# Two edits to one kernel: the last steps of the attention part written out by hand, and the Mish reciprocal computed by three squares and one cubic step in halves

## The chip, the cores and the metric

One core of a Trainium2 chip runs the whole kernel. The metric is the device time of one execution in microseconds (us), lower is better. The median of the kernel before is 1624.23 us over 3 runs, from 1624.13 to 1624.23.

## What is computed

The reference is a transformer-like block on 64 graphs of 128 nodes and 384 features, in float32. Cut to what matters:

```python
x = x + attention(layernorm(x), adj)        # 12 heads of 32, adj is added to the scores, softmax
x = x + moe(layernorm(x))                   # below, layernorm of its output with gain and offset

pooled = u.mean(axis=1)                     # one routing decision for each graph
logits = pooled @ router_w.T + router_b     # 4 experts, the best 2 are taken
h = act[e](u @ w1[e] + b1[e])               # 384 -> 768; act = gelu, silu, mish, gelu
out = h @ w2[e] + b2[e]                     # 768 -> 384
y = gate-weighted sum of the 2 + u
mish(v) = v * tanh(softplus(v))
```

## The kernel before

The kernel is written for each engine by hand, with semaphores between the engines. `act.wait_ge(s, n)` stops only that engine's own list until the semaphore `s` has reached `n`; what is behind it in the list waits too. Matrices are split in a high and a low part, and each product is three matmuls (`split_product`, L495).

**Attention part.** The loop `for h in STEPS` runs over the 64 graphs (B = 64, graphs 0 to 63) as a software pipeline: in step h an engine works on the scores of graph h, on the probabilities of graph h-1, on the output projection of graph h-2 and on the normalised tile `u` of graph h-3. The names are: `exps` (ScalarE, L776, 12 exponentials for a graph), `take_probs` (copy of the transposed probabilities, two of three tiles on ScalarE at L795, the third on VectorE at L1206), `take_inverse` (L806), `divide` (VectorE, L1225 to L1231), `project_o` (TensorE), `residual` (VectorE, L1196 to L1201), `root2` (GpSimd, L1073 to L1077), `normalise_x1` (ScalarE, L783, writes `u` into `xu`), `transpose_u` (TensorE, L601), `take_u` (ScalarE, L801), `sum_nodes` (VectorE, L1218). Each graph's `xu` (384 KB) is stored to DRAM from the SP queue (L425) and so is its transposed `u` (192 KB, L397).

**Weights under dead tiles.** The expert part's tiles lie over those of the attention part. As the last graphs leave tiles, ScalarE's DMA queue loads into them: four `w1_hi` parts of 1152 KB (L824), the bias `b1_wide` of 1536 KB (L844) and six pieces of `w2_both` (L829; 896, 1920, 2560, 1152, 768 and 1920 KB). The functions `load_under_...` hold the waits for that, and stand in ScalarE's list between its activations.

**Expert part.** There are 128 jobs, two for each graph: job (b, k). TensorE's list for a job is six transposes of an activated tile (`transpose_act`, L704), the 18 matmuls of `first_layer` of a later job, and the 18 of `second_layer` of this one. VectorE adds the bias (`take_hidden`, L1323), ScalarE and VectorE apply the activation, ScalarE and VectorE split the transposed tile in `at_hi` (L998) and `at_lo` (L1402). The expert of a job is read at run time, and `If` picks the activation. In this run 17 jobs are Mish jobs.

**The Mish job before.** ScalarE computes a tanh and a square that give the number whose reciprocal is wanted, and then a seed by two squares (L916, L1005). VectorE then does three operations on the whole 128x768 tile (L1430, L1433, L1437), with one square of ScalarE (L1007) beside the second, and at the end the product in two halves (L1441):

```python
nc.scalar.activation(inverse[:], inverse[:], ACT.Square, bias=seed_out[:]).then_inc(seed_done, 1)
act.wait_ge(miss_done, i + 1)
nc.scalar.activation(miss2[:], half_t[:], ACT.Square, scale=-1.0, bias=one_col[:]).then_inc(miss2_done, 1)
```

The first job, (0, 0), starts on ScalarE only when several things are there: the routing, the last output projection, and the stores of the `xu` tiles of graphs 60 and 61, over which its tiles lie (`xu_stored[0]`):

```python
act.wait_ge(routed, 1)
act.wait_ge(wo_mm, B)
for g in range(2):
    act.wait_ge(xu_stored[0][g], 16 * stored(0))
activate(0, 0, choice(0, 0))
```

## Time and profile before

| | |
|---|---|
| median of 3 runs | 1624.23 us |
| the profiled execution's own time | 1624.92 us |
| its span | 1623.0 us |
| granted TensorE clock, mean | 0.997 |
| busy: TensorE, VectorE, ScalarE, GpSimd | 1587.8, 1193.3, 971.5, 687.3 us |

The profiled execution is 0.69 us above the median, and 1.92 us of its time lie outside the span. Times in the views are microseconds from the span's start; durations in the grouped view are in nanoseconds. In a row of the timeline the bracket gives how long the engine sat idle before it and what released it. TensorE runs at 2.4 GHz where the granted clock reads 1.00, and at 1.2 GHz where it reads 0.50.

### The profile page before, as it was taken

Reading aid. Unit: us, or ns where it says so; the run is one execution under the profiler, and the core shown is the slowest. Engines: PE = TensorE matmul, PEld = TensorE weight load, DVE = VectorE, ACT = ScalarE, POOL = GpSimd, SP = SyncE. Lnnn points to the kernel's source line nnn. Section 1 sums busy time; section 2 is a strip of 40 time slices with the busy share of each in tenths; the row PEclk is TensorE's granted clock in tenths of the full one; section 3 lists DMA queues with packets and bytes.
Section 4 is the critical chain, followed back from the end, with each engine's and each line's share of the span. In section 5 each row is a group of like instructions: output and inputs, shape, how many; then the busy total and the mean of one; then the engine's idle time right before and its main releaser. Section 6 shows DMA issues by size and latency. Waiting matters only on the chain.

```text
span 1623.0 us, 44743 instructions
## 1 busy us (share of the span) xinstructions
PE 1587.8 (98%) x12720; PEld 1524.2 (94%) x12720; DVE 1193.3 (74%) x3752; ACT 971.5 (60%) x2882; POOL 687.3 (42%) x1105
## 2 busy tenths in 40 slices
PE   7999999999999999979999999999999999999998
PEld 7999999999999999879999999999999999999998
DVE  5788788878888788767766666776777767677776
ACT  6899999998999988853433333443444434343442
POOL 3777887778877887631111111111111111111112
PEclk9999999999999999999999999999999999999999
DMA  5433333344444433582111111122211111111211
GB/s 186 157 118 125 109 115 115 127 158 153 153 154 161 151 121 120 221 312 85 52 59 60 58 57 60 60 60 61 61 60 45 58 58 60 60 60 50 66 50 45
DMA packets 93511, 163.87 MB, mean 101 GB/s; under 512 B 10304, under 2 KB 73792, under 8 KB 92096
## 3 DMA queue, kind: packets, MB, share of 16 engines
q1 hardware_dynamic: 91664, 145.01, 27.3%
q10 hardware_dynamic: 1584, 15.73, 2.6%
q8 instruction: 119, 1.95, 0.5%
q14 instruction: 144, 1.18, 0.2%
HBM read 96.22 MB, written 64.49 MB: 99 GB/s over the span
## 4 chain that ended last, share of the span: by engine, by line
PE 88%; DVE 5%; ACT 2%; issue 2%; DMA 1%; POOL 1%; DVEq 1%; ACTq 0%; POOLq 0%; SPq 0%
PE bank L495 67%; PE bank L569 5%; PE bank L704 5%; PE bank L522 3%; PE bank L592 3%; PE bank L609 2%; PE bank L578 1%; PE bank L601 1%; DVE inverse L1437 1%; DVE half_t L1430 1%; DVE inverse L1433 1%; ACT inverse L1005 1%; ACT at_hi L998 1%; DMA xu_scratch<-xu 1%; ACT prob L776 1%
## 5 line engine op out<-in xcount | busy, mean ns | idle before, releaser
L495 PE MATMUL bank<-w_hi,ut_in 128*128 x1536 | 421.3, 341 | 0.1
L495 PE MATMUL bank<-w_both,at_hi 128*128 x1524 | 388.8, 335 | 8.0 <-DVE at_lo L1402 7.3
L776 ACT ACTIVATE prob<-att,heads 128x128 f32<-128x128 f32 x768 | 297.6, 394 | 15.0 <-DVE heads L1166 12.1
L495 PEld LDWEIGHTS bank<-w_both,at_hi 128*128 128x128 f32 x1524 | 274.3, 188 | 13.6 <-issue 13.6
L495 PEld LDWEIGHTS bank<-w_hi,ut_in 128*128 128x128 f32 x1536 | 279.5, 188 | 1.1 <-issue 1.1
L495 PE MATMUL bank<-w_lo,ut_in 128*128 x768 | 257.0, 335 | 0.0
L495 PE MATMUL bank<-w_both,at_lo 128*128 x762 | 255.1, 335 | 0.0
L920 ACT ACTIVATE hid<-hid 128x384 f32<-128x384 f32 x192 | 95.0, 526 | 257.1 <-DVE hid L1323 254.9
L998 ACT ACTIVATE at_hi<-bank,gate_col 128x384 fp32r<-128x384 f32 x254 | 133.4, 576 | 192.5 <-PE bank L704 190.5
L1142 POOL TENSOR_TENSOR xz<-xz,lnb_wide 128x384 f32<-128x384 f32 x64 | 67.9, 1062 | 403.7 <-DVE xz L1468 383.7
L1402 DVE SCALAR_TENSOR_TENSOR at_lo<-bank,gate_col,at_hi 128x384 fp32r<-128x384 f32 x254 | 144.7, 611 | 113.4 <-ACT at_hi L998 113.3
L1323 DVE TENSOR_TENSOR hid<-bank,b_wide 128x384 f32<-128x384 f32 x256 | 130.7, 552 | 118.1 <-PE bank L495 107.7
L1130 POOL TENSOR_SCALAR rs_z<-mv_z 128x1 f32<-128x1 f32 x64 | 40.8, 638 | 346.0 <-DVE mv_z L1456 346.0
L1166 DVE CUSTOM_DVE_ANT_0 att<-bank,adj_in 128x128 f32<-128x128 f32 x768 | 171.7, 286 | 12.5 <-PE bank L522 12.0
L495 PE MATMUL bank<-xt_hi,wt_hi 128*128 128x256 f32 x576 | 169.1, 294 | 0.1
L495 PE MATMUL bank<-xt_lo,wt_hi 128*128 128x256 f32 x576 | 162.6, 282 | 0.0
L495 PE MATMUL bank<-xt_hi,wt_lo 128*128 128x256 f32 x576 | 162.6, 282 | 0.0
L776 ACT ACTIVATION_READ_ACCUMULATOR prob<-att,heads 128x1 f32 x768 | 147.7, 192 | 0.0
L495 PEld LDWEIGHTS bank<-w_lo,ut_in 128*128 128x128 f32 x768 | 144.7, 188 | 0.0
L495 PEld LDWEIGHTS bank<-w_both,at_lo 128*128 128x128 f32 x762 | 143.0, 188 | 0.0
L1088 POOL TENSOR_TENSOR fold<-att 128x768 f32<-128x768 f32 x64 | 117.2, 1832 | 0.0
L495 PEld LDWEIGHTS bank<-xt_hi,wt_hi 128*128 128x128 f32 x576 | 109.6, 190 | 7.6 <-issue 0.4
(139 smaller groups left out, 3485.8 us busy)
## 6 DMA issues: line engine op xcount, KB each, us to landing
xu_scratch<-xu SPq DMA_DIRECT2D x64, 384.0 KB, 2.3
xz<-xu_scratch SPq DMA_DIRECT2D x64, 384.0 KB, 3.2
x_in<-in_x SPq DMA_DIRECT2D x32, 384.0 KB, 3.2
xu<-in_x SPq DMA_DIRECT2D x32, 384.0 KB, 4.2
ut_scratch<-ut_out SPq DMA_DIRECT2D x64, 192.0 KB, 1.9
ut_in<-ut_scratch SPq DMA_DIRECT2D x64, 192.0 KB, 2.4
out_dram<-xz SPq DMA_DIRECT2D x64, 192.0 KB, 1.9
w_lo<-in_L_ffn_w SPq DMA_DIRECT2D x4, 1152.0 KB, 6.3
```

What stands on the lines that cost most here:

```text
L495: last = nc.tensor.matmul(acc, lhs[c][a], rhs[c][b], start=start and n == 0, stop=stop and n == len(terms) - 1)
L522: last = nc.tensor.matmul(bank[r][:, c * N:(c + 1) * N], q_t[p][rows, c, cols], k_t[p][rows, c, cols], start=True, stop=True)
L569: last = nc.tensor.transpose(bank[c][:, i * N:(i + 1) * N], prob[n % 2][:, c * HPB + i, :], ident[:])
L704: last = nc.tensor.transpose(banks[c // DC][:, (c % DC) * P:(c % DC + 1) * P], hid[k][:, c // DC, (c % DC) * P:(c % DC + 1) * P], ident[:])
L776: nc.scalar.activation(prob[g][:, hh, :], att[g][:, head, :], ACT.Exp, bias=neg_max[g][:, head:head + 1], scale=-1.0, accum_out=row_sum[g] ...
L920: nc.scalar.activation(hid[k][:, s], hid[k][:, s], ACT.Gelu).then_inc(a_ready[k], 1)
L998: nc.scalar.activation(flat(hi[:, s * DC:(s + 1) * DC, :]), banks[s][:, 0:HALF], ACT.Copy, scale=gate_col[:, col, 1:2]).then_inc(at_hi_don ...
L1088: nc.gpsimd.tensor_tensor(fold[:], att[g][:, :, 0:width], att[g][:, :, width:N], ALU.add).then_inc(fold_done, 1)
L1142: nc.gpsimd.tensor_tensor(x1, x1, lnb_wide[:], ALU.add).then_inc(x_based, 1)
L1166: last = nc.vector.tensor_tensor_reduce(out=att[g][:, head, :], in0=bank[r][:, c * N:(c + 1) * N], in1=adj_in[p][:, g, :], scale=-1.0, sca ...
L1323: nc.vector.tensor_tensor(hid[k][:, s], hid_ps[k][s][:, 0:HALF], b1_wide[:].rearrange("p e s f -> p (e s f)")[:, bass.ds(e * F + s * HALF, ...
L1402: nc.vector.scalar_tensor_tensor(out=flat(lo[:, s * DC:(s + 1) * DC, :]), in0=banks[s][:, 0:HALF], scalar=gate_col[:, col, 1:2], in1=flat( ...
```

## The change

First, the last steps. The three loops of ScalarE, VectorE and GpSimd stop early (after h = 62, 62 and 63), and what is left is written out in a new order. On TensorE the order stays but for `transpose_u(61)`, which moves behind the first layer of job (0, 0). Two of three probability copies of graph 62 move from ScalarE to VectorE. `normalise_x1(60)` moves ahead of the exponentials of graph 63, `load_under_residuals` too, and that function now loads `b1_wide` in place of a part of `w1_hi`; this part is loaded four steps earlier, since `x_in` and `xu2` trade places in memory. GpSimd adds the output bias of graph 62 ahead of `guard_sums(63)`.

Second, the Mish jobs. The seed is made with three squares in place of two, and then one cubic step in place of the steps before: VectorE has three operations in halves (six instructions of 384 columns) where it had three whole ones and two halves, and ScalarE's `miss2` comes in halves.

```diff
-        xu = [sb("xu2", [P, 2, 2, D], F32, s1)]
+        x_in = [sb(f"x_in{p}", [P, 2, D], F32, s1) for p in range(2)]
...
+            normalise_x1(B - 4)
+            load_under_residuals()
+            exps(B - 1, (0, 1, 2, 3))
+            take_inverse(B - 2)
+            load_under_scores()
+            take_probs(B - 1, 0)
+            take_probs(B - 1, 1)
+            take_u(B - 4)
+            load_under_exps()
+            round_ut(0, 0, 0)
+            load_under_probs()
+            nc.scalar.preload_act_table(ACT.Gelu)
+            take_inverse(B - 1)
+            round_ut(1, 1, 0)
+            normalise_x1(B - 3)
+            load_under_attended()
+            normalise_x1(B - 2)
+            take_u(B - 3)
+
+            act.wait_ge(routed, 1)
+            act.wait_ge(wo_mm, B)
+            for g in range(2):
+                act.wait_ge(xu_stored[0][g], 16 * stored(0))
+            activate(0, 0, choice(0, 0))
+            normalise_x1(B - 1)
+            take_u(B - 2)
...
-                    nc.scalar.activation(inverse[:], inverse[:], ACT.Square, bias=seed_out[:]).then_inc(seed_done, 1)
-                    act.wait_ge(miss_done, i + 1)
-                    nc.scalar.activation(miss2[:], half_t[:], ACT.Square, scale=-1.0, bias=one_col[:]).then_inc(miss2_done, 1)
+                    nc.scalar.activation(inverse[:], inverse[:], ACT.Square, scale=SEED[1][0], bias=seed_mid[:]).then_inc(seed_more, 1)
+                    act.wait_ge(seed_more, i + 1)
+                    nc.scalar.activation(inverse[:], inverse[:], ACT.Square, scale=SEED[2][0], bias=seed_out[:]).then_inc(seed_done, 1)
+
+                    for s in range(2):
+                        act.wait_ge(miss_done, 2 * i + s + 1)
+                        nc.scalar.activation(miss2[:, s], half_t[:, s], ACT.Square, scale=-1.0, bias=miss_col[:]).then_inc(miss2_done, 1)
...
+            add_bias_and_max(B - 1, (0, 1, 2, 3))
+            invert_sums(B - 2)
+            for c in range(PTC):
+                take_probs(B - 2, c)
+            residual(B - 3)
+            divide(B - 2)
+            greatest_part(B - 1)
+            take_probs(B - 1)
+            invert_sums(B - 1)
+            rest_of_ut(0, 0, 0)
+            sum_nodes(B - 4)
+            residual(B - 2)
+            divide(B - 1)
...
-                    nc.vector.scalar_tensor_tensor(out=half_t[:], in0=half_t[:], scalar=1.0, in1=inverse[:],
-                                                   op0=ALU.add, op1=ALU.mult).then_inc(miss_done, 1)
...
                     for s in range(2):
+                        nc.vector.scalar_tensor_tensor(out=half_t[:, s], in0=half_t[:, s], scalar=1.0, in1=inverse[:, s],
+                                                       op0=ALU.add, op1=ALU.mult).then_inc(miss_done, 1)
+                    for s in range(2):
+                        dve.wait_ge(miss2_done, 2 * i + s + 1)
+                        nc.vector.scalar_tensor_tensor(out=inverse[:, s], in0=miss2[:, s], scalar=0.75, in1=inverse[:, s],
+                                                       op0=ALU.add, op1=ALU.mult).then_inc(newton_done, 1)
+                    for s in range(2):
+                        dve.wait_ge(newton_done, 2 * i + s + 1)
```

ScalarE's list from the last exponentials of graph 62 on, before:

```order
L776 ACTIVATE prob0,heads<-att0,heads 128x128 x6
L776 ACTIVATE prob1,heads<-att1,heads 128x128 x12
L783 ACTIVATE xu0<-xu0,norms 128x384
L795 ACTIVATE pt0<-bank0 128x512
L795 ACTIVATE pt1<-bank1 128x512
L824 DMA w1_hi<-w1h_scratch 128x2304
L829 DMA w2_both<-w2_scratch 128x5120
L887 ACTIVATE ut_in0<-ut_in0 128x384
L801 ACTIVATE ut_out0<-bank3 128x384
L806 ACTIVATE inv_t<-bank5 128x384
```

The same place of the changed kernel (`prob` are exponentials, `xu` the normalised tile, `pt` the copies of probabilities, `inv_t` the copy of the inverse sums):

```order
L783 ACTIVATE prob0,heads<-att0,heads 128x128 x6
L790 ACTIVATE xu0<-xu0,norms 128x384
L868 DMA b1_wide<-in_L0_ffn_b1 128x3072
L783 ACTIVATE prob1,heads<-att1,heads 128x128 x12
L813 ACTIVATE inv_t<-bank5 128x384
L836 DMA w2_both<-w2_scratch 128x5120
L802 ACTIVATE pt0<-bank0 128x512
L802 ACTIVATE pt1<-bank1 128x512
L808 ACTIVATE ut_out0<-bank3 128x384
```

The normalised tile of graph 60 and the DMA of the bias now stand ahead of the 12 exponentials of graph 63, and the two copies of graph 62 are gone from this list.

VectorE's list behind the inverse sums of graph 62, before:

```order
L1196 TENSOR_TENSOR xu0<-bank6,xu0 128x384
L1199 BN_STATS norms<-xu0 128x6
L1201 BN_AGGR norms<-norms 128x2
L1206 COPY pt2<-bank2 128x512
L1218 TENSOR_REDUCE pooled<-bank3 128x3
L1225 TENSOR_TENSOR ot0<-bank4,inv_t 128x384
```

And in the changed kernel:

```order
L1226 COPY pt0<-bank0 128x512
L1226 COPY pt1<-bank1 128x512
L1226 COPY pt2<-bank2 128x512
L1216 TENSOR_TENSOR xu0<-bank6,xu0 128x384
L1219 BN_STATS norms<-xu0 128x6
L1221 BN_AGGR norms<-norms 128x2
L1245 TENSOR_TENSOR ot0<-bank4,inv_t 128x384
```

All three copies of graph 62 now come ahead of the residual of graph 61, and `sum_nodes(60)` (`pooled`) has moved to a later place.

ScalarE's list of a Mish job after its first two squares, in the changed kernel:

```order
L1013 ACTIVATE inverse<-inverse,seed_mid 128x768
L1015 ACTIVATE inverse<-inverse,seed_out 128x768
L1019 ACTIVATE miss2<-half_t,miss_col 128x384 x2
```

The line with `seed_mid` is new; before there was one whole square with `seed_out` and one whole `miss2`.

## Rows read from the trace of the kernel before

**Rows 1.** The page: busy time of each engine.
```profile
PE 1587.8 (98%) x12720; PEld 1524.2 (94%) x12720; DVE 1193.3 (74%) x3752; ACT 971.5 (60%) x2882; POOL 687.3 (42%) x1105
```
**Rows 2.** Busy time by stretch, with granted clock, DMA share and GB/s last.
```profile
700.00:720.00 20.00, 17.90 (x133) 16.12 (x132) 11.37 (x25) 8.01 (x15) 6.47 (x14) 0.85 0.98 394
...
800.00:1600.00 800.00, 793.71 (x4799) 784.20 (x4799) 559.74 (x1132) 306.69 (x571) 130.67 (x172) 1.00 0.19 58
```
**Rows 3.** The chain that ended last, in order of time: start, length, what.
```profile
709.52 8.86 DMA xu_scratch<-xu
```
**Rows 4.** Timeline of TensorE, from graph 62 to job (0, 1).
```profile
699.74 0.90 PE L601 MATMUL bank<-ident,xu 128*128 128x128 f32 x3 [2.35 <-ACT xu L783]
...
711.54 0.44 PE L495 MATMUL bank<-w_hi,ut_in 128*128 x1
...
726.22 0.61 PE L495 MATMUL bank<-w_both,at_hi 128*128 x2 [1.59 <-DVE at_lo L1402]
...
731.43 0.93 PE L704 MATMUL bank<-ident,hid 128*128 128x128 f32 x6 [1.16 <-DVE hid L1441]
```
**Rows 5.** Timelines of ScalarE (ACTq: its DMA issues), GpSimd, SP's queue and VectorE.
```profile
694.36 0.40 ACT L776 ACTIVATE prob<-att,heads 128x128 f32<-128x128 f32 x1 [1.08 <-DVE heads L1166]
...
698.99 0.69 ACT L783 ACTIVATE xu<-xu,norms 128x384 f32<-128x384 f32 x1
...
711.60 0.33 ACTq L829 DMA_DIRECT2D w_both<-w_scratch  x1
...
719.62 0.94 ACT L920 ACTIVATE hid<-hid 128x384 f32<-128x384 f32 x2 [2.27 <-issue]
...
726.04 0.94 ACT L1005 ACTIVATE inverse<-inverse,seed_out 128x768 f32<-128x768 f32 x1
...
696.49 0.26 POOL L1077 TENSOR_SCALAR norms<-norms 128x1 f32<-128x1 f32 x1
...
689.12 0.32 SPq L425 DMA_DIRECT2D xu_scratch<-xu  x1
...
727.71 0.95 DVE L1430 SCALAR_TENSOR_TENSOR half_t<-half_t,inverse 128x768 f32<-128x768 f32 x1
```
**Rows 6.** DMA issues (KB, us to landing) near 711, 689 and 713, and a stretch.
```profile
w_both<-w_scratch ACTq DMA_DIRECT2D x1, 1920.0 KB, 12.9
...
xu_scratch<-xu SPq DMA_DIRECT2D x1, 384.0 KB, 6.8
...
xu_scratch<-xu SPq DMA_DIRECT2D x1, 384.0 KB, 12.1
...
697.50:724.50 27.00, 22.46 (x160) 20.42 (x160) 13.16 (x30) 14.15 (x31) 8.81 (x16) 0.87 0.92 361
```
**Rows 7.** Timeline of two Mish jobs of one graph, TensorE, ScalarE and VectorE.
```profile
1422.29 0.99 ACT L912 ACTIVATE half_t<-hid 128x384 f32<-128x384 f32 x2 [2.36 <-DVE hid L1323]
...
1424.51 0.82 PE L704 MATMUL bank<-ident,hid 128*128 128x128 f32 x6
...
1426.31 0.93 ACT L1005 ACTIVATE inverse<-inverse,seed_out 128x768 f32<-128x768 f32 x1
...
1430.30 1.03 DVE L1441 SCALAR_TENSOR_TENSOR hid<-inverse,hid 128x384 f32<-128x384 f32 x2
1431.41 0.82 PE L704 MATMUL bank<-ident,hid 128*128 128x128 f32 x6
...
1440.45 0.93 PE L704 MATMUL bank<-ident,hid 128*128 128x128 f32 x6 [0.82 <-DVE hid L1441]
...
1448.19 0.82 PE L704 MATMUL bank<-ident,hid 128*128 128x128 f32 x6
```
**Rows 8.** Groups from 740 us on, and all L704 matmuls behind 738 us.
```profile
L1441 DVE SCALAR_TENSOR_TENSOR hid<-inverse,hid 128x384 f32<-128x384 f32 x32 | 16.4, 554 | 0.6
...
L1430 DVE SCALAR_TENSOR_TENSOR half_t<-half_t,inverse 128x768 f32<-128x768 f32 x16 | 15.3, 958 | 2.4 <-ACT inverse L1005 2.4
...
L704 PE MATMUL bank<-ident,hid x756: 269/272/329, 738.5 to 1609.5; 128*128 128x128 f32 x189
```

More of the change, by code:

```diff
@@ L95, in gnn_moe_kernel @@
             wt_lo.append(sb(f"wt_lo{m}", [P, DC, D], F32R, s1))
-        x_in = [sb(f"x_in{p}", [P, 2, D], F32, s1) for p in range(2)]
+        xu = [sb("xu2", [P, 2, 2, D], F32, s1)]
         xt_hi = [sb("xt_hi0", [P, DC, 2 * N], F32R, s1)]
@@ L843, in load_under_projections @@
                     load_w1_hi(2)
-                    act.dma_start(b1_wide[:].rearrange("p e s f -> p (e s f)"), b1.rearrange("(o e) f -> o (e f)", o=1).partition_broadcast(P)).then_inc(b1_loaded, 16)
                 if h == B - 3:
@@ L859, in load_under_residuals @@
                 act.wait_ge(ut_mm, B - 4)
-                load_w1_hi(1)
+                act.dma_start(b1_wide[:].rearrange("p e s f -> p (e s f)"), b1.rearrange("(o e) f -> o (e f)", o=1).partition_broadcast(P)).then_inc(b1_loaded, 16)
             def load_under_scores():
@@ L915, in activate @@
                         act.wait_ge(square_done, i + 1)
-                        nc.scalar.activation(inverse[:], half_t[:], ACT.Square, scale=SEED_G ** 0.5, bias=seed_in[:]).then_inc(seed_half, 1)
+                        nc.scalar.activation(inverse[:], half_t[:], ACT.Square, scale=SEED[0][0], bias=seed_in[:]).then_inc(seed_half, 1)
                     with act.Else():
@@ L923, in activate @@
                         act.sem_inc(seed_half, 1)
-            for h in STEPS:
+            for h in range(STEPS.start, B - 1):
                 if h == B - 2:
                     load_under_values()
-                if h == B + 1:
-                    load_under_attended()
                 if 0 <= h - 2 < B - 3:
                     round_o(h - 2)
-                if h == B:
-                    nc.scalar.preload_act_table(ACT.Gelu)
                 if has(h + 4):
@@ L943, in _ @@
                     exps(h, (0, 1))
-                if h == B - 1:
-                    exps(h, (2, 3))
-                if h == B + 2:
-                    act.wait_ge(routed, 1)
-                    act.wait_ge(wo_mm, B)
-                    for g in range(2):
-                        act.wait_ge(xu_stored[0][g], 16 * stored(0))
-                    activate(0, 0, choice(0, 0))
-                if has(h - 3) and h != B:
+                if has(h - 3):
                     normalise_x1(h - 3)
@@ L960, in _ @@
                     take_probs(h - 1, 1)
-                if h == B:
+                if has(h - 3):
+                    take_u(h - 3)
+                if has(h - 1):
                     take_inverse(h - 1)
-                    normalise_x1(h - 3)
-                if h == B - 1:
-                    load_under_residuals()
-                    load_under_scores()
-                    round_ut(0, 0, 0)
-                if h == B:
-                    round_ut(1, 1, 0)
-                if h == B:
-                    load_under_probs()
-                if has(h - 3) and h not in (B, B + 2):
-                    take_u(h - 3)
-                if has(h - 1) and h != B:
-                    take_inverse(h - 1)
-                if h == B:
-                    take_u(B - 3)
                 if has(h + 5):
@@ L985, in _ @@
                     round_weights(3)
-                if has(h) and h != B - 1:
+                if has(h):
                     exps(h, (2, 3))
-                if h == B - 1:
-                    load_under_exps()
+            normalise_x1(B - 4)
[23 more added lines that the diff above has]
+            take_u(B - 2)
             def split_act_hi(b, k, m):
@@ L1107, in add_output_bias @@
                 nc.gpsimd.tensor_tensor(xu[p][:, g, 0, :], xu[p][:, g, 0, :], bo_wide[:], ALU.add).then_inc(xbo_done, 1)
-            for h in STEPS:
+            for h in range(STEPS.start, B):
                 if 0 <= h - 2 < B - 3:
@@ L1123, in _ @@
                     root1(h + 6)
+            add_output_bias(B - 2)
+            guard_sums(B - 1)
+            root2(B - 3)
+            add_output_bias(B - 1)
+            root2(B - 2)
+            root2(B - 1)
             pool.wait_ge(routed, 1)
@@ L1343, in route_first_half @@
                     route_gates(0)
-            for h in STEPS:
+            for h in range(STEPS.start, B - 1):
                 if h == -4:
@@ L1376, in _ @@
                     rest_of_weights(3)
-                if has(h - 3) and h not in (B, B + 2):
+                if has(h - 3):
                     sum_nodes(h - 3)
@@ L1393, in _ @@
                     greatest_part(h)
+            add_bias_and_max(B - 1, (0, 1, 2, 3))
+            invert_sums(B - 2)
+            for c in range(PTC):
+                take_probs(B - 2, c)
[8 more added lines that the diff above has]
+            divide(B - 1)
+            rest_of_ut(1, 1, 0)
+            dve.wait_ge(routed, 1)
+            dve.wait_ge(o_mm, B)
+            dve.wait_ge(b1_loaded, 16)
+            take_hidden(0, 0, 0, 0, choice(0, 0))
+            residual(B - 1)
+            sum_nodes(B - 3)
+            take_hidden(0, 1, 0, 0, choice(0, 1))
+            sum_nodes(B - 2)
             def split_act_lo(b, k, m):
```

105 lines of the change are left out of this document (46 added, 59 removed).

## The prediction

> **What bounds the kernel now.** I read the page first, then the busy time by stretch, then the chain that ended last, and then the timelines where the chain leaves TensorE. The page gives TensorE 1587.8 us of a span of 1623.0 [rows 1], so all its idle time together is 35 us, and much of that is at the start and the end. The stretches show two places where an edit off TensorE can be worth anything. From 700 to 720 TensorE is busy for 17.90 of 20 us at a mean clock of 0.85, with the DMA engines full (0.98 of their time, 394 GB/s); from 800 to 1600 it is busy for 793.71 of 800 us [rows 2]. The first place is the change from attention to experts, the second is where the Mish jobs are. The two halves of the change go to these two places, and I cost them apart.
>
> **Where the change-over is bound.** TensorE has gaps of 2.35 us before the transposes of graph 60's `u` at 699.74, 1.59 before the second layer of job (0, 0) at 726.22 and 1.16 before the transposes of job (0, 1) at 731.43 [rows 4]. But the gaps before 712 don't set the end by themselves: the chain runs for 8.86 us, from 709.52 on, through one store of an `xu` tile [rows 3]. That is graph 61's store; job (0, 0) may not be activated before it has landed. It lands at 718.4, the Gelu of job (0, 0) starts at 719.62 after the choice of its expert has been read [rows 5], and TensorE transposes its result 0.6 us later. I call the start of this Gelu G.
>
> **The change-over with the new order.** Step by step:
> - `normalise_x1(60)` ran at 698.99, behind the 12 exponentials of graph 63 that began at 694.36. Its input, GpSimd's `root2(60)`, is ready at 696.49 + 0.26 = 696.75 [rows 5]. It now runs at 696.8, and TensorE's transposes of it move from 699.74 to about 697.5. The price is that the exponentials stand behind it: they begin at 697.4, 3.0 us later, and with their 4.6 us (694.36 to 698.99) end at 702.0.
> - The copies of graph 62 on VectorE let `attend(62)` run some 3 us earlier, which pays for the late exponentials. Behind them come the inverse copy of graph 62 (702.5), `divide(62)` on VectorE (to about 704.1), the projection of graph 62, the inverse sums of graph 63 and `attend(63)`. Carrying the durations of before through the new lists, I get the first layer of job (0, 0) at about 707.4 where it was at 711.54 [rows 4], and that of job (0, 1) done at 716.1, some 3.7 us earlier. TensorE would be ready for the transposes of (0, 0) at 716.4 in place of about 720. These are sums of some ten steps, estimates good to perhaps a microsecond.
> - The gate is the store of graph 61. `normalise_x1(61)` ends at about 708.0, so the store is issued there in place of 709.52: 1.5 us earlier. It doesn't land 1.5 us earlier, though. The store of graph 60's transposed `u` is ahead of it on the SP queue and now issues 1 us later (`take_u(60)` is behind the late exponentials), while the same large loads of `w2_both` share the engines, which are full [rows 2]. The bounds are two other `xu` stores near it: 6.8 us to landing for the one issued at 689.12, 12.1 us for the one near 713 [rows 5, 6]. So it lands between 714.8 and 720.1; I take 718.0, since the backlog is nearly that of before. G is then 719.2, 0.4 us earlier.
> - The second gate is the last load of `w2_both`, needed by the second layer of (0, 0) at 726.22 [rows 4]. It landed 12.9 us after its issue at 711.6 [rows 5, 6], at 724.5. Its issue now comes at 708.8, but what counts is the volume ahead of it. From 697.5 on the queue now carries `b1_wide` (1536 KB) where it carried a part of `w1_hi` (1152 KB): 384 KB more, at 361 GB/s over that stretch [rows 6] 1.1 us, of which about 0.6 us come back since the queue no longer runs dry before the 2560 KB load. I take 725.0: no gate, but with only 0.8 us to spare. At the 394 GB/s of the stretch up to 720 [rows 2] all of it (27 us x 361 GB/s + 0.39 MB = 10.1 MB) would have passed by 723.3.
> - Job (0, 1) is the first Mish job. VectorE started on it at 727.71 though ScalarE's seed was done at 726.98 [rows 5]; so the added square costs only 0.97 - 0.73 = 0.24 us here, while VectorE's part is shorter (below: 2.74 us to the first half of the result in place of 3.61). It gains 0.6 us net. With G 0.4 us earlier, its transposes go from 731.43 to 730.4. **Term: -1.0 us.** Both bounds: with the store at 714.8 and the loads at 723.3 TensorE and the Mish chain of (0, 1) are the limit, 727.5, and the sum is -3.9; with the store at 720.1 it is 1.7 - 0.6 = +1.1.
>
> **The Mish jobs.** From 740 us on there are 16. In each one VectorE waits for ScalarE's seed, 0.15 us (2.4 us in 16) [rows 8], so the seed is on the path, and the jobs are late for TensorE: transposes come every 6.90 us (1424.51 to 1431.41), but 9.04 and 7.74 us apart where both jobs of a graph are Mish [rows 7]. Over the part: 756 transposes are 126 jobs, the first at 738.5, the last two together at about 1608.3 (the last matmul starts at 1609.5) [rows 8]. 124 steps of 6.90 us are 855.6, the stretch is 869.8: 14.2 us are lost, and all that I looked at follow Mish jobs. So what a Mish job takes longer goes to the end 1:1, 16 times.
> - Before: from the end of the seed (1426.31 + 0.93 = 1427.24) to the end of the last product (1430.30 + 1.03 = 1431.33) are 4.09 us [rows 7].
> - Added: a whole square on ScalarE, 0.93 and 0.04 to the next, 0.97 us. Nothing hides it, since VectorE is already waiting.
> - VectorE's part now: one half takes 0.554 us alone [rows 8] and two together 1.03 [rows 7], so the second starts 0.48 after the first. The two misses end at 0.58 and 1.06; ScalarE's halves (two in 0.99 us, as the tanh [rows 7]) at 1.15 and 1.63; the next two of VectorE at 1.78 and 2.26; the last two at 2.74 and 3.22.
> - Sum: 0.97 + 3.22 = 4.19 in place of 4.09, 0.10 us later. **Term: 16 x 0.10 = +1.6 us.** Bounds: the four hand-overs free, -0.05 a job, -0.8 us; no overlap between halves (0.58 each with its wait, so 3.56 us), 0.44 a job, +7.0 us.
>
> The Trainium skill, "VectorE: DVE Perf Modes", section "The TRN2 errata", speaks against halving: a fixed cost for each instruction whose source is in SBUF, (N+151) cycles at 0.96 GHz, is paid for each small tile. By that page 384 columns are 557 ns and 768 are 957; the trace agrees on single instructions (554 and 958). By its rule two halves would be 1.11 us, where the trace has 1.03 for two in a row; with nothing overlapping, a job would come out as in the third rival.
>
> Other edits cost nothing: the constants, two more semaphore increments in other jobs, and the earlier load of `w1_hi`, which lies under steps in which TensorE never waits.
>
> **Sum.** 1624.92 - 1.0 + 1.6 = 1625.5 against the profiled execution, which is 0.69 us above the median: 1624.8 us. A measurement of this kernel can tell 0.2%, 3.25 us, from no change; so I forecast no change, between 1620.98 and 1627.48.
>
> **Rivals.**
> 1. *The forecast*, each half worth a microsecond or two and of opposite sign: 1624.8, alone from 1622 to 1627.4. Chance 0.66.
> 2. *The change-over really gets short*: the store lands early because its queue is empty, and the loads run at 394 GB/s throughout. For it speaks that TensorE is ready 3.6 us earlier; against it, that the same bytes must pass the same engines. -3.9, and with Mish at -0.8 to +1.6 it is 1620.2 (to 1622). Chance 0.15, and it counts as faster from -3.25 on.
> 3. *The halves do not overlap where a semaphore stands between them*, so a Mish job is 0.44 us later: -1.0 + 7.0 = 1630.2, slower. It decides from 0.27 us a job on (16 x 0.27 - 1.0 = 3.3). Against it: two halves in 1.03 us. For it: those two had no waits between them that were still open. Chance 0.13. The rule of the page named above leads here.
> 4. *ScalarE gets stuck ahead of the exponentials of graph 63*: the list now waits there for the store of graph 59, issued at 689.12. It landed after 6.8 us at 695.9 [rows 5, 6], 0.9 us before `root2(60)` is ready. If it took the 12.1 us of the slow one [rows 6], the exponentials and all behind them were 4.4 us late, which takes the 3.7 us back and more: about 1627 to 1629. Chance 0.06, half of it slower.
>
> **Chances and range.** Faster 0.16, same 0.66, slower 0.18 (rival 3, half of rival 4 and the edge of the forecast). The range from 1621.0 to 1628.5 leaves out most of rival 3 and the best of rival 2.
>
> **What would show it.** Right: the first layer of (0, 0) near 707.4 and done twice by 716.1; a store of graph 61 issued near 708 that lands at 718, with ScalarE's Gelu again the releaser of the transposes of (0, 0) and a gap of some 3 us before them; VectorE waiting 1.1 us for the seed in each Mish job; paired Mish jobs 0.2 us later than the 9.04 + 7.74 of before. Wrong: no gap before the transposes of (0, 0) (rival 2), a wait of the second layer for a `w2_both` load (my DMA sum is off), six VectorE halves in more than 3.4 us (rival 3), or ScalarE idle after 697.5 with a DMA as the releaser (rival 4).

## The result, and the profile after

The changed kernel takes 1627.39 us (median of 20 runs, 1625.54 to 1628.58) where the kernel before takes 1624.99 us in the same series (20 runs, 1623.92 to 1626.29). The ratio is 1.0014, with a 95% interval of 1.0008 to 1.002. So it is slower by about 2.4 us, which is real, but below the 0.2% that I had set as no change. The forecast was 1624.8 us, 2.6 us too low. In the experiments below, one of the 12 executions of `halves_packed` took 2608.34 us at a granted clock of 0.557, and its ratio leaves that one out.

The profiled execution has a span of 1625.1 us, 2.1 us above that of before. The page, to be held against [rows 1], has nearly the same for TensorE and GpSimd; ScalarE has 32 instructions and 18 us more, VectorE 14 us less:

```profile
PE 1589.0 (98%) x12720; PEld 1525.0 (94%) x12720; DVE 1179.2 (73%) x3771; ACT 989.8 (61%) x2914; POOL 688.9 (42%) x1106
```

The two stretches of [rows 2], and behind them one around the first transposes of an expert job:

```profile
700.00:720.00 20.00, 14.96 (x109) 13.28 (x108) 11.33 (x27) 9.55 (x24) 6.17 (x13) 0.99 1.01 418
717.50:724.50 7.00, 5.99 (x27) 5.62 (x27) 1.12 (x3) 5.75 (x11) 0.00 (x0) 0.76 0.78 321
800.00:1600.00 800.00, 792.68 (x4783) 782.63 (x4782) 544.38 (x1140) 321.74 (x597) 130.04 (x171) 1.00 0.19 58
```

The reader is to see three things. TensorE is busy for less of the change-over (14.96 us of 20 in place of 17.90), since it has done its part sooner and waits. It ran there at full clock (0.99 in place of 0.85), and the low clock has moved behind it: 0.76 from 717.5 to 724.5, where before it was 1.00. And from 800 to 1600 us TensorE is busy 1.03 us less and does 16 matmuls fewer, so the expert part has become longer.

**The change-over.** Below are the chain through the store (as in [rows 3]), the timeline of TensorE at the places of [rows 4], and the rows of ScalarE, VectorE and SP's queue that belong to [rows 5].

```profile
707.58 9.00 DMA xu_scratch<-xu
```
```profile
696.97 0.55 PE L604 MATMUL bank<-ident,xu 128*128 128x128 f32 x3 [0.16 <-ACT xu L790]
...
707.21 0.44 PE L497 MATMUL bank<-w_hi,ut_in 128*128 x1 [0.39 <-issue]
...
718.38 0.96 PE L711 MATMUL bank<-ident,hid 128*128 128x128 f32 x6 [2.40 <-ACT hid L928]
...
724.82 0.62 PE L497 MATMUL bank<-w_both,at_hi 128*128 x2 [0.44 <-DVE at_lo L1434]
...
729.65 0.93 PE L711 MATMUL bank<-ident,hid 128*128 128x128 f32 x6 [0.75 <-DVE hid L1471]
```
```profile
696.21 0.71 ACT L790 ACTIVATE xu<-xu,norms 128x384 f32<-128x384 f32 x1 [3.51 <-POOL norms L1091]
...
707.58 0.32 SPq L427 DMA_DIRECT2D xu_scratch<-xu  x1
...
708.14 0.33 ACTq L836 DMA_DIRECT2D w_both<-w_scratch  x1
...
715.80 1.02 DVE L1343 TENSOR_TENSOR hid<-bank,b_wide 128x384 f32<-128x384 f32 x2 [1.77 <-PE bank L497]
...
717.80 0.94 ACT L928 ACTIVATE hid<-hid 128x384 f32<-128x384 f32 x2 [4.77 <-DVE hid L1343]
718.64 0.69 ACT L790 ACTIVATE xu<-xu,norms 128x384 f32<-128x384 f32 x1
719.24 0.47 ACT L808 ACTIVATE ut_out<-bank 128x384 f32<-128x384 f32 x1
720.56 0.94 ACT L920 ACTIVATE half_t<-hid 128x384 f32<-128x384 f32 x2 [0.85 <-issue]
...
725.75 0.94 ACT L1015 ACTIVATE inverse<-inverse,seed_out 128x768 f32<-128x768 f32 x1
...
726.73 1.03 DVE L1463 SCALAR_TENSOR_TENSOR half_t<-half_t,inverse 128x384 f32<-128x384 f32 x2 [0.33 <-ACT inverse L1015]
```

All of this execution runs 0.58 us early already before any changed step: the transposes of the probabilities of graph 62 start at 695.75, where they started at 696.33. With that taken off, the transposes of job (0, 1) come 1.20 us earlier (731.43 to 729.65 is 1.78), where I had forecast 1.0. The Gelu of job (0, 0) still waits for the store of graph 61; the releaser that the row names, VectorE's `hid`, was done at 716.82, and the store landed at 707.58 + 9.00 = 716.58, behind which the choice has to be read. In the traces of all 13 kernels of this document the Gelu starts 1.22 to 1.24 us after this store has landed, whenever `hid` was done, so the store is the gate in each of them.

**The Mish jobs.** The groups from 740 us on, to be held against [rows 8]:

```profile
L1019 ACT ACTIVATE miss<-half_t,miss_col 128x384 f32<-128x384 f32 x32 | 18.0, 610 | 10.0 <-DVE half_t L1463 10.0
L1467 DVE SCALAR_TENSOR_TENSOR inverse<-miss,inverse 128x384 f32<-128x384 f32 x32 | 17.1, 558 | 3.5 <-ACT miss L1019 3.5
L1463 DVE SCALAR_TENSOR_TENSOR half_t<-half_t,inverse 128x384 f32<-128x384 f32 x32 | 16.4, 555 | 18.0 <-ACT inverse L1015 18.0
L1471 DVE SCALAR_TENSOR_TENSOR hid<-inverse,hid 128x384 f32<-128x384 f32 x32 | 16.3, 552 | 0.0
L1015 ACT ACTIVATE inverse<-inverse,seed_out 128x768 f32<-128x768 f32 x16 | 15.0, 938 | 0.5
```

VectorE waits 18.0 us in 16 jobs for the seed, 1.12 each (0.15 before), and 3.5 us, 0.22 each, for the first half of the miss, where the steps of the forecast leave some 0.14 (from 1.06 to 1.20). The pair of Mish jobs of [rows 7] in the new kernel:

```profile
1431.64 1.02 DVE L1471 SCALAR_TENSOR_TENSOR hid<-inverse,hid 128x384 f32<-128x384 f32 x2
1432.87 1.02 DVE L1343 TENSOR_TENSOR hid<-bank,b_wide 128x384 f32<-128x384 f32 x2 [0.21 <-issue]
...
1438.18 0.94 ACT L1015 ACTIVATE inverse<-inverse,seed_out 128x768 f32<-128x768 f32 x1
1439.15 1.03 DVE L1463 SCALAR_TENSOR_TENSOR half_t<-half_t,inverse 128x384 f32<-128x384 f32 x2 [1.12 <-ACT inverse L1015]
1439.75 1.13 ACT L1019 ACTIVATE miss<-half_t,miss_col 128x384 f32<-128x384 f32 x2 [0.63 <-DVE half_t L1463]
1440.40 1.07 DVE L1467 SCALAR_TENSOR_TENSOR inverse<-miss,inverse 128x384 f32<-128x384 f32 x2 [0.21 <-ACT miss L1019]
1441.38 1.02 DVE L1471 SCALAR_TENSOR_TENSOR hid<-inverse,hid 128x384 f32<-128x384 f32 x2
...
1442.08 0.92 PE L711 MATMUL bank<-ident,hid 128*128 128x128 f32 x6 [1.01 <-DVE hid L1471]
```

From the end of the seed (1439.12) to that of the last product (1442.40) are 3.28 us, so with the added square 4.25 in place of 4.09. I then took the start of the transposes of every job and summed what the distances have over 6.90 us, from job (0, 1) to the last: 14.4 us before (731.43 to 1608.33), 18.2 after (729.65 to 1610.38). With -0.58 and -1.20 that is +2.0 us, the 2.1 of the spans.

The 3.8 us are of three kinds. The first distances of the three Mish pairs have 2.60 to 2.62 over 6.90 in place of 2.14 to 2.17, together +1.4; the second ones are as before. The ten single Mish jobs have together some 1.1 more. And 1.3 us lie where nothing was changed: of the 107 distances that don't start at a Mish job ("plain jobs" below), nearly half are 6.92 or 6.93 us in place of 6.90.

### The profile page after: what moved, and what is told of

It reads as the page before. It is cut to its first block, busy times and chain, and to the rows that moved or that the text cites. A ratio compares the mean times of both kernels' runs of the same rounds, so it can differ in the third digit from the quotient of the medians.

```text
span 1625.1 us, 44838 instructions
## 1 busy us (share of the span) xinstructions
PE 1589.0 (98%) x12720; PEld 1525.0 (94%) x12720; DVE 1179.2 (73%) x3771; ACT 989.8 (61%) x2914; POOL 688.9 (42%) x1106
## 3 DMA queue, kind: packets, MB, share of 16 engines
q8 instruction: 119, 1.95, 0.5%
## 4 chain that ended last, share of the span: by engine, by line
PE 88%; ACT 4%; DVE 4%; issue 2%; DMA 1%; DVEq 1%; POOL 0%; ACTq 0%; POOLq 0%; SPq 0%
PE bank L497 67%; PE bank L572 5%; PE bank L711 5%; PE bank L524 3%; PE bank L595 3%; PE bank L612 2%; PE bank L581 1%; PE bank L604 1%; ACT inverse L1015 1%; ACT inverse L1013 1%; ACT at_hi L1006 1%; ACT miss L1019 1%; DMA xu_scratch<-xu 1%; DVE inverse L1467 1%; DVE half_t L1463 1%
## 5 line engine op out<-in xcount | busy, mean ns | idle before, releaser
L497 PEld LDWEIGHTS bank<-w_both,at_hi 128*128 128x128 f32 x1524 | 274.2, 188 | 13.7 <-issue 13.7
L1186 DVE CUSTOM_DVE_ANT_0 att<-bank,adj_in 128x128 f32<-128x128 f32 x768 | 171.7, 287 | 12.4 <-PE bank L524 11.9
```

What stands on the lines that cost most here:

```text
L497: last = nc.tensor.matmul(acc, lhs[c][a], rhs[c][b], start=start and n == 0, stop=stop and n == len(terms) - 1)
L1186: last = nc.vector.tensor_tensor_reduce(out=att[g][:, head, :], in0=bank[r][:, c * N:(c + 1) * N], in1=adj_in[p][:, g, :], scale=-1.0, sca ...
```

## The experiments

Each run has the kernel before beside it on the same chip, and the diffs are written in short form; "excess" is the sum over 6.90 us just described. For the change-over I give the distance D from the transposes of the probabilities of graph 62 to those of job (0, 1): 35.10 us before (731.43 - 696.33), 33.90 in the changed kernel (729.65 - 695.75). The starts are these rows, of before and of after:

```profile
696.33 1.06 PE L569 MATMUL bank<-ident,prob 128*128 128x128 f32 x8 [0.99 <-ACT prob L776]
695.75 1.07 PE L572 MATMUL bank<-ident,prob 128*128 128x128 f32 x8 [1.02 <-issue]
```

Spans of single executions are a coarser measure: the transposes of graph 62, ahead of which only one load has moved, start anywhere between 694.85 and 696.93 us.

**Each half of the change alone.** `tail_only` is the changed kernel with the old Mish code (the two tables and the loop of the Mish part as before); `mish_only` the converse.

> The written-out last steps alone, with the Mish jobs of before. Theory A (the two halves of the change are additive, the last steps gain and the Mish jobs lose): about 1.2 to 1.8 us faster than before (ratio 0.9989 to 0.9993), the transposes of job (0, 1) near 730 and the jobs after it spaced as before, 14.4 us above 6.90 us each. Rival B (the last steps are worth nothing, their lead is lost again): ratio 1.000 within 0.0004. Rival C (the plain jobs became 0.02 us longer because of the last steps, say by where tiles lie): every second plain job takes 6.92 us here too.

Measured: 1624.39 us, ratio 0.9995 (0.9986 to 1.0004); excess 14.5, plain jobs 6.90, D = 34.36. Rival C is out. The interval holds both a gain of 1.2 us and none, so A and B are not told apart by the time.

> The new Mish jobs alone, with the last steps of before. Theory A: slower by what the spacing of the transposes shows, 3.8 us less 0.6 us that the first Mish job gains: ratio 1.0017 to 1.0024, and every second plain job at 6.92 us if that belongs to the Mish code. Rival B (the Mish jobs are neutral and the loss is from elsewhere): ratio 1.000 within 0.0005.

Measured: 1628.26 us, ratio 1.002 (1.0011 to 1.0029); excess 18.6, plain jobs 6.92 to 6.93 as in the changed kernel, D = 33.63. The two ratios add up to that of the whole change. The loss belongs to the Mish part, and the odd 0.02 us in jobs without Mish come with it too. That D is the shortest here, with the old last steps, was expected by nothing. The profiled execution is the fastest of the 11 (1626.14 us, mean granted clock 0.999); eight others have a mean clock of 0.996 or 0.997 and took 1628.18 to 1629.37 us, so this D is not that of a typical execution.

**The halving undone.** `whole_tiles` keeps the added square and the cubic step and works on whole tiles:

```
-for s in range(2): act.wait_ge(miss_done, 2*i + s + 1); miss2[:, s] = Square(half_t[:, s])
+act.wait_ge(miss_done, i + 1); miss2 = Square(half_t)
-for s in range(2): half_t[:, s] = ...    # and the same for the product that follows
+half_t[:] = ...
```

> The changed kernel with the cubic step on whole tiles (three VectorE steps, the last in halves, miss2 whole): the halving alone is undone. Theory A (what a Mish job takes longer goes to the end one to one, 16 times): the chain behind the seed is 0.03 + 0.96 + 0.04 + 0.94 + 0.04 + 0.96 + 0.03 + 1.03 = 4.03 us in place of 3.28, so 0.75 us x 16 = 12 us slower than the changed kernel, ratio to before about 1.009. Rival (the halves gain nothing, since small tiles cost more, or the jobs have slack): within 2 us of the changed kernel, ratio 1.001 to 1.003.

Measured: 1638.9 us, ratio 1.0087 (1.0071 to 1.0102); excess 28.1. Its group behind 740 us shows where the time goes, ScalarE and VectorE in turn:

```profile
L1464 DVE SCALAR_TENSOR_TENSOR inverse<-miss,inverse 128x768 f32<-128x768 f32 x16 | 15.3, 959 | 16.1 <-ACT miss L1018 16.1
```

The wait for the miss is 1.01 us a job where the halves leave 0.22. So the halves do overlap across a semaphore, and rival 3, which said that they don't, is out. The passage of Mish time to the end can be read here too. The chain of a job is 0.73 us longer (4.98 - 4.25), but VectorE then pauses 0.09 us ahead of the next job's bias where in the changed kernel it pauses 0.21, so 0.61 us a job or 9.8 us should pass on; the excess is 9.9 higher. (The span is 11.9 us longer, since D is 1.2 us longer as well, 35.11, and the execution 0.8 us late before any changed step.)

**The seed in halves.** `half_seed` extends the halving by one step back:

```
-inverse = Square(inverse, seed_mid); act.wait_ge(seed_more, i + 1)
-inverse = Square(inverse, seed_out)
+for s in range(2): inverse[:, s] = Square(inverse[:, s], seed_mid)
+for s in range(2): act.wait_ge(seed_more, 2*i + s + 1); inverse[:, s] = Square(inverse[:, s], seed_out)
```

> The changed kernel with the second and third square of the seed in halves too, so that VectorE starts on the first half while ScalarE does the second. Theory A (the seed is on the path): the first half of the seed is there 0.45 us earlier, a Mish job is 0.4 us shorter, 16 x 0.4 = 6 us faster than the changed kernel, ratio to before 0.997 to 0.998. Rival (VectorE's second halves then wait for ScalarE, which is the bound, and nothing is gained): ratio 1.0014 as the changed kernel.

Measured: 1622.22 us, ratio 0.998 (0.9971 to 0.9989), span 1619.5; excess 13.7, D = 33.70. It is faster than both kernels. The first distances of the pairs are 2.02 to 2.05 over 6.90, 0.57 less than in the changed kernel. The excess has fallen by 4.5 us, 0.28 a job and not the expected 0.4: ScalarE's four halves take 2.13 us together where its two whole squares took 1.90. The other 1.1 us of the span are D (0.2) and an early start (0.9). VectorE waits less for the seed:

```profile
L1465 DVE SCALAR_TENSOR_TENSOR half_t<-half_t,inverse 128x384 f32<-128x384 f32 x32 | 17.1, 558 | 13.4 <-ACT inverse L1017 13.4
```

**The added square priced alone.** `no_added_square` leaves out the line with `seed_mid`.

> The changed kernel without the square that it adds to the seed (the one with seed_mid), so that the reciprocal starts from a coarser seed and its output is less exact; all else is there. It prices the added square alone. Theory, that VectorE waits for the seed and the square is on the path in each Mish job (0.97 us each): first jobs of the three pairs lose 0.7 us in place of 2.6, the single ones nothing or up to 0.3, so the sum over 6.90 falls from 18.2 to about 8 and the span to 1615 us, ratio 0.995. Rival, that something else is late in most Mish jobs (the wait of 0.21 us for the misses, the read of the choice): the sum falls by less than 5 us.

Measured: 1616.1 us, ratio 0.9946 (0.9932 to 0.996), span 1613.7; excess 6.7. The wait for the seed is nearly gone:

```profile
L1462 DVE SCALAR_TENSOR_TENSOR half_t<-half_t,inverse 128x384 f32<-128x384 f32 x32 | 16.4, 555 | 2.5 <-ACT inverse L1014 2.2
```

The square costs 11.4 us of span in 16 jobs, 0.7 each on average. VectorE waits 15.5 us less for the seed, 0.97 a job, which is the whole square. A pair gets it back in full: its first distance has 0.66 over 6.90, 1.95 less for two jobs. A single Mish job gets back only what it was late, 0.54 us on average, and is then on time. The kernel leaves out a step of the reciprocal, so this is a price and not a version to use.

**The odd hundredths in jobs without Mish.** The added tile `seed_mid` takes 32 bytes of each partition in the built program (a figure of the build, which no trace shows), so every tile allocated behind it lies that much further on. `seed_packed` puts the two bias columns in one tile, `tail_padded` is `tail_only` with an unused column:

```
-seed_in = sb("seed_in", [P, 1]); seed_mid = sb("seed_mid", [P, 1])
+seed_cols = sb("seed_cols", [P, 2])          # seed_packed, on the changed kernel
+sb("pad_col", [P, 1])                        # tail_padded, on tail_only
```

> The changed kernel with its two bias columns seed_in and seed_mid in one tile of two columns, so that every later SBUF tile lies at the address that it has in the kernel before; nothing else changes. In both kernels with the new Mish code, every second job without Mish takes 6.92 to 6.93 us where it takes 6.90 in the kernel before and in tail_only; both have the extra tile. Theory that the 32 bytes of shift are the cause: all plain jobs take 6.90 us and the sum of job times over 6.90 falls from 18.2 to about 17 us, the time by 1.2 us. Rival, that it comes from the new code in each job (more semaphore increments and instructions in the branches that jobs without Mish take): nothing changes, 6.92 to 6.93 and 18.2 stay.

Measured: 1626.32 us, ratio 1.0011 (1.0002 to 1.002). The 107 plain jobs are together 0.1 us over 6.90 where the changed kernel has 1.3, and the excess is 17.0.

> The kernel of tail_only (last steps written out, old Mish code) with one unused column more, which moves all later SBUF tiles by 32 bytes; it is the converse of seed_packed. Theory of the addresses: every second plain job takes 6.92 to 6.93 us, and the sum over 6.90 rises from 14.5 by about 1.2 us. Rival, the new code in each job: 6.90 and 14.5 stay.

Measured: 1624.88 us, ratio 1.0 (0.9991 to 1.0009). The plain jobs are 1.5 us over 6.90 where `tail_only` has 0.0, and the excess is 15.8. Two neighbouring jobs of it, 6.93 us apart; a few matmuls of the first layer, right behind the transposes, take up to 346 ns in place of 334 and follow each other up to 0.01 us later:

```profile
802.73 0.82 PE L710 MATMUL bank<-ident,hid 128*128 128x128 f32 x6
...
809.66 0.82 PE L710 MATMUL bank<-ident,hid 128*128 128x128 f32 x6
```

So the shift makes it, both ways, and the new code does not. It is not all loss: over 28 graphs of attention (from about 305 to 606 us) all kernels with the shift take 300.08 or 300.09 us and those without 300.27 or 300.28, some 0.4 us over the whole part. The total effect of below 1 us is less than the intervals of the ratios can tell.

**The gate at the change-over.** `swap_store` lets SP issue the store of graph 61's `xu` ahead of the store of graph 60's transposed `u`:

```
 sp.dma_start(xu_dram[n], xu[...])
-if n < B - 1: store_ut(n)
+if n == B - 3: store_ut(n - 1)
+if n < B - 1 and n != B - 4: store_ut(n)
```

> The changed kernel, but SP issues the store of graph 61's xu ahead of the store of graph 60's transposed u. Theory, that the store of graph 61 is the gate of the first expert job and is late because of what lies ahead of it on SP's queue: it lands near 715 in place of 716.6, the choice can be taken sooner, and the transposes of job (0, 0) come 1 to 2 us before 718.38; those of job (0, 1) come at about 728 in place of 729.65, unless the last w2 load (landing 722.7) stops it. Rival, that the DMA engines are full and order on one queue does not matter: it lands at 716.6 all the same and nothing moves by more than 0.3 us.

Measured: 1628.44 us, ratio 1.0024 (1.0015 to 1.0033), span 1626.9; D = 35.80. ScalarE behind the Gelu, and TensorE:

```profile
717.32 0.94 ACT L930 ACTIVATE hid<-hid 128x384 f32<-128x384 f32 x2 [4.13 <-DVE hid L1345]
718.16 0.69 ACT L792 ACTIVATE xu<-xu,norms 128x384 f32<-128x384 f32 x1
719.55 0.49 ACT L810 ACTIVATE ut_out<-bank 128x384 f32<-128x384 f32 x1 [0.69 <-DMA ut_scratch<-ut_out]
721.99 0.94 ACT L922 ACTIVATE half_t<-hid 128x384 f32<-128x384 f32 x2 [1.95 <-issue]
```
```profile
726.24 0.61 PE L499 MATMUL bank<-w_both,at_hi 128*128 x2 [3.92 <-DVE at_lo L1436]
```

And the busy time by stretch, with the granted clock third from the end:

```profile
726.50:730.50 4.00, 4.00 (x15) 4.00 (x15) 3.59 (x9) 2.56 (x4) 0.00 (x0) 0.57 0.85 287
```

The store of graph 61 lands 8.4 us after its issue in place of 9.0, and the Gelu comes 0.6 us earlier (717.32 against 717.80 in an execution that is 0.16 us late). So it is the gate, and the order on SP's queue counts for 0.6 us, not for the microsecond or two that I expected. But the other store, now behind, keeps the buffer of transposed `u`: ScalarE's copy waits 0.69 us for it, and the idle time behind it, in which the choice of job (0, 1) is read, is 1.95 us in place of 0.85 (why it is longer, no row shows). The tanh of job (0, 1) starts at 721.99 in place of 720.56. ScalarE's `at_hi` of job (0, 0) stands behind the tanh and two squares, so the second layer starts 4.25 to 4.26 us after the tanh in all 13 kernels, and TensorE waits 3.92 us in place of 0.44. It then runs this layer mostly at 1.2 GHz (granted clock 0.57), and from its start to the transposes of (0, 1) are 5.47 us in place of 4.83. So the gain of 0.6 at the store has turned into a loss of 1.9 in D: 1.9 lost on ScalarE and 0.6 in the second layer at the low clock. The medians agree in sign (1.0024 against 1.0014), but the intervals of the two ratios overlap.

**All edits together.** `halves_packed_swap` is `half_seed` with packed columns and the swapped stores; `halves_packed` is the same without the swap.

> The changed kernel with three edits: the second and third squares of the seed in halves too (as half_seed), the bias columns packed (as seed_packed), and the xu store of graph 61 first (as swap_store). If the gains add, it is half_seed's 1619.5 us of span less 1.2 (addresses) and less 0 to 1 (store, part of which half_seed already had, its job (0, 1) being transposed at 728.55): 1617.3 to 1618.3 us of span, 1619 to 1621 as a median, ratio 0.996 to 0.998. If the addresses and the store order are worth nothing it is half_seed's 1622.

Measured: 1623.85 us, ratio 0.9991 (0.9982 to 1.0), not the 0.996 to 0.998 expected. Excess 12.2 as hoped for, but the swap again costs more than it gives: D = 38.70. The profiled execution is the slowest of the 11 (1626.87 us), so its D is not typical. In it TensorE waits 2.96 us for `at_lo` at 728.95 and then runs the whole second layer at half clock:

```profile
725.00:735.00 10.00, 7.04 (x26) 6.77 (x25) 6.48 (x15) 7.63 (x15) 0.00 (x0) 0.66 0.62 223
```

> half_seed with its two bias columns packed in one tile, and SP's stores in the order of the changed kernel. Theory that gains add: Mish part as half_seed (12.2 us over 6.90 a job in Mish jobs), plain jobs at 6.90 (1.3 to 1.5 us less over the expert part), attention about 0.4 us longer, since its steps are that much shorter with the shifted tiles. So it is half_seed less about 1 us: ratio 0.997, 1621 us. Rival, that the shift is worth as much in attention as it costs in the experts: 1622, the ratio of half_seed (0.998).

Measured: 1621.76 us, ratio 0.9977 (0.9968 to 0.9986), span 1619.9; excess 12.4, D = 33.72. This is the best version here, though `half_seed` (0.998) can't be told from it.

**The written-out steps on the better base.** `old_steps_halves_packed` has the Mish code of `halves_packed` and the last steps of the kernel before.

> The same Mish code and packed columns as halves_packed, but the last steps of attention in the order of the kernel before. It tells what the written-out steps are worth once the Mish code is good. In mish_only the transposes of job (0, 1) came 33.6 us behind those of the probabilities of graph 62, in the changed kernel 33.9, in tail_only 34.4, in the kernel before 35.1. Theory, that the written-out steps no longer gain with the new Mish code: within 0.5 us of halves_packed, ratios within their intervals. Rival, that they are worth their 0.7 us or more on any base: it is 0.7 to 1.2 us slower than halves_packed.

Measured: 1623.21 us, ratio 0.9988 (0.9979 to 0.9997), span 1622.2; excess 12.8, D = 35.41. It is 1.5 us slower than `halves_packed` on the same chip, in the direction of the rival; the intervals of the two ratios overlap, so this is likely, not settled.

**What the written-out steps are worth.** D can be taken apart, since two of its pieces are the same in all kernels: 1.22 to 1.24 us from the landing of graph 61's store to the Gelu, and 4.25 to 4.26 from the tanh of (0, 1) to the second layer of (0, 0). The other pieces, in us; the store's times count from the transposes of graph 62:

| kernel | last steps | store issued | store landed | Gelu to tanh | second layer to transposes of (0, 1) | D |
|---|---|---|---|---|---|---|
| before | old | 13.19 | 22.06 | 2.34 | 5.21 | 35.10 |
| `mish_only` | old | 12.86 | 21.36 | 2.09 | 4.69 | 33.63 |
| `old_steps_halves_packed` | old | 12.97 | 21.88 | 2.58 | 5.46 | 35.41 |
| `tail_only` | new | 11.84 | 20.90 | 2.76 | 5.22 | 34.36 |
| changed | new | 11.83 | 20.83 | 2.76 | 4.83 | 33.90 |
| `halves_packed` | new | 11.84 | 20.93 | 2.90 | 4.41 | 33.72 |

The new order lands the store 0.4 to 1.2 us earlier and gives 0.2 to 0.8 us back between Gelu and tanh, where its list has one copy more. What is left depends on where the low clock falls. Here are `mish_only` and `old_steps_halves_packed` from 725 to 732 us, where the second layer of the latter lies, and a row of that layer:

```profile
725.00:732.00 7.00, 6.37 (x41) 6.11 (x40) 5.58 (x13) 4.03 (x8) 0.00 (x0) 1.00 0.52 172
725.00:732.00 7.00, 5.32 (x23) 5.33 (x24) 5.94 (x14) 4.75 (x10) 0.00 (x0) 0.76 0.58 192
```
```profile
729.93 0.84 PE L496 MATMUL bank<-w_both,at_hi 128*128 x2
```

Two such matmuls take 0.51 us at full clock. Of the 1.78 us by which D differs between these two kernels with the same last steps, 0.5 are the store's landing, 0.5 the idle time ahead of the tanh and 0.8 the second layer at the low clock. The medians point the same way, though not cleanly: of the 83 executions of the kernel before that stand beside the experiments, the 21 with a mean clock of 0.999 have a median of 1624.3 us, the 13 at 0.998 one of 1625.7 and the 49 at 0.996 or 0.997 one of 1625.4; `tail_only`, always at 0.998 or more, took 1624.4. So the gain of about 1 us that the medians give the written-out steps may be a low-clock stretch less, and not shorter steps. No run here holds the clock still to tell.

## Why the prediction was near, and where it was off

**The number.** Of the 2.6 us, 0.8 are the base: the kernel before has a median of 1624.99 us over 20 runs where the forecast started from 1624.23 over 3. The change itself was forecast at +0.6 us and measured at +2.4.

**What bounds the kernel.** Right in both places: the change-over ends on the store of graph 61, and Mish time goes to the end, with one limit that the forecast left out. What passes on is the chain and VectorE's pause behind it together (`whole_tiles`), and a job passes on a saving only as long as it is late (`no_added_square`).

**The steps of the change-over.** With the 0.58 us of the early start added to the times of after, they were near: transposes of graph 60's `u` at 697.55 (forecast 697.5), first layer of (0, 0) at 707.8 (707.4), store issued at 708.2 (708.0). The landing was mis-sized: 9.0 us from issue, not the 10.0 that I took between the bounds of 6.8 and 12.1, so G came at 718.4 and not at 719.2. The last `w2_both` load landed 14.6 us after its issue at 708.14, at 722.7 (723.3 in the time of before), which is the value that I had worked out from 394 GB/s and not the 725.0 that I took; it gated nothing.

**The first Mish job, a wrong step that the one above made good.** I let job (0, 1) gain 0.6 us behind G. It gained nothing: G came 1.24 us earlier and the transposes 1.20. VectorE's shorter part gave the expected 0.8 (from 726.73 to 729.65 are 2.92 us, 3.72 before), and the added square cost 0.97 - 0.69 = 0.28. What I left out is a ScalarE instruction: the written-out list puts the copy of graph 62's transposed `u` (719.24) between the Gelu and the tanh of (0, 1), and from the one to the other are 2.76 us where [rows 5] and the tanh of before, at 721.96, give 2.34. The rest is 0.13 us of small gaps on ScalarE. The term of -1.0 came out as -1.2, close by luck: the store was taken 0.8 us too late and the job 0.6 us too short. And it is the difference of two single executions, with the low clock in different places (0.53 from 699.5 to 706.5 before, 0.76 from 717.5 to 724.5 after).

**The Mish term was mis-sized, +1.6 forecast, +3.8 measured.** Three errors of one sign:
- The jobs themselves lost 2.5 us, not 1.6. The chain behind the seed is 3.28 us, not 3.22, since two of ScalarE's halves with its column bias take 610 ns each (1.12 us in a row), not the 0.99 that I took from the tanh. That makes 0.16 a job in place of 0.10, 2.6 us if all of it passed.
- VectorE's next job starts 0.21 us after the products where in pairs it started at once (1431.33 to 1431.41, second row below), 0.13 more. In a pair both jobs' lateness comes out in the first distance, 2 x 0.16 + 0.13 = 0.45, which is what all three pairs show. Single jobs scatter between -0.1 and +0.5, for the most part with this pause: in five of the ten it was 0.45 us before, and in four of these it is 0.21 now, so they lose nothing.
- The 32 bytes of the new tile, 1.3 us here. I had written that the constants cost nothing.

Two rows of the kernel before to this: the tanh of job (0, 1), and VectorE's bias of the second job of the pair.

```profile
721.96 0.94 ACT L912 ACTIVATE half_t<-hid 128x384 f32<-128x384 f32 x2 [0.80 <-DVE hid L1323]
1431.41 1.02 DVE L1323 TENSOR_TENSOR hid<-bank,b_wide 128x384 f32<-128x384 f32 x2
```

With them the sum is -1.2 + 3.8, and the early start of 0.6 us (part of it from the same shift) leaves the +2.0 of the spans.

**The price of small tiles.** In a row two halves take 1.02 to 1.07 us, and the halving makes the chain of a job 0.73 us shorter here, since it lets two engines work at the same time. The rule that the prediction took from the Trainium skill, "VectorE: DVE Perf Modes", section "The TRN2 errata", holds again for a single instruction: 384 columns take 552 to 558 ns, 557 by an estimate from the page's formula. Added up, it would have led to rival 3, which the trace does not bear out.

**The rivals.** Rival 2 (-3.9) is out: the store landed earlier than taken, at 717.2 in the time of before, but neither at 714.8 nor with an empty queue; by its own terms its sum was 1619.5 to 1621.9, not 1620.2 to 1622. Rival 3 is out by `whole_tiles`. Its bound was set too high: six times 0.58 us are 3.48, not 3.56, so 0.36 a job and +5.8 us. Rival 4 did not occur: ScalarE ran `normalise_x1(60)` at 696.21, right when GpSimd had its input ready.

**What stays open.** What decides where the low clock falls, and so whether the written-out steps are worth their microsecond. With them D was 33.7 to 34.6 us in seven kernels (`whole_tiles` and the two with swapped stores apart), with the old ones 33.6, 35.1 and 35.4, one execution each. Why the idle time ahead of the tanh differs between kernels is open too. And why tiles shifted by 32 bytes delay some matmuls was not looked for.

## What to carry to other kernels

Where two engines hand a tile back and forth, add up the chain in both ways before adding precision: cutting the tile in halves shortened the chain by 0.73 us here, the added whole square cost 0.7 a job, and cutting that square too was what made the change pay. An instruction that the critical engine's list puts between two steps of the chain counts at its full length, even where its own result is not urgent, and a transfer that is moved forward on a queue moves another one back: look at who needs that one. A microsecond read from one execution on each side may be the clock: compare the granted clock of the same stretch, and the medians, before naming a cause. When a change of well below 1% is judged, add no tile without a look at what it shifts.

## What was not expected of the hardware

- Moving all tiles by 32 bytes changes the rhythm of TensorE: 6.90 us a job become 6.92 to 6.93 in about half of them, while attention gets 0.19 us shorter in 300 (28 graphs). Shown in both directions, on otherwise equal programs.
- ScalarE's squares on 128x384, with a column bias and two in a row, take 608 to 611 ns each, its Gelu and tanh on the same shape, without a column, some 526; a whole 128x768 square with a column takes 938. Whether the function or the column makes the difference, no run here separates.
- The stretch in which TensorE runs at 1.2 GHz is not tied to a step: it lay between 699.5 and 706.5 before (granted clock 0.53), behind a gap of 2.35 us, and in the 7 us from 717.5 on after (0.76), behind one of 2.40. With the swapped stores it lay in the second layer of (0, 0): 0.57 from 726.5 to 730.5 behind a gap of 3.92 us, and 0.66 from 725 to 735 behind one of 2.96.
- The idle time in which ScalarE reads an expert's number between two instructions is 0.56, 0.85 and 1.04 us in three kernels, and 1.22 and 1.95 us in the two where a wait for a DMA stands ahead of it. How much of it is the read is not shown.
